# Two-layer graph network on one core: moving the second layer's epilogue one unit later

## The reference

```python
def _L0_gnn_ref(h, adj, W_neigh, b_neigh, W_self, b_self):
    deg = jnp.sum(adj, axis=1, keepdims=True) + 1e-05
    h_neigh = (adj / deg) @ h
    return relu(h_neigh @ W_neigh.T + b_neigh + h @ W_self.T + b_self)

def _L1_gnn_ref(x, adj, W, b):
    d = jnp.where(adj.sum(axis=1) > 0, adj.sum(axis=1) ** (-0.5), 0.0)
    support = (d[:, None] * adj * d[None, :]) @ x
    return relu(support @ W + b)

x = _layernorm(x + _L0_gnn_ref(x, adj, ...))
x = _layernorm(x + _L1_gnn_ref(x, adj, W, b))
```

## Time and profile before

| | |
|---|---|
| profiled execution | 786.03 us, span 784.3 us |
| median of three runs | 786.57 us |
| PE busy | 769.7 us (98%) |
| DVE busy | 719.4 us (92%) |
| ACT busy | 422.7 us (54%) |
| second layer | from about 418 us |
| its inner blocks (1 to 6) | about 448 to 722 us |
| two squarings (line 399), mean of one | 468 ns |
| one normalisation (line 405), mean | 589 ns |

### The profile page before, as it was taken

One profiled execution on the slowest core, in us unless ns is written; L12 is line 12 of the kernel. 1 busy time (PEld: TensorE's weight loads), 2 busy tenths in 40 slices (PEclk: granted clock), 3 DMA queues, 4 the chain that ended last, 5 costly groups with the idle time before them and its releaser, 6 DMA issues.

```text
span 784.3 us, 12479 instructions
## 1 busy us (share of the span) xinstructions
PE 769.7 (98%) x4050; PEld 658.7 (84%) x4050; DVE 719.4 (92%) x1221; ACT 422.7 (54%) x590; POOL 2.6 (0%) x14
## 2 busy tenths in 40 slices
PE   9999999999999999999999999999999999999996
PEld 6888888888888888888888789898888889888886
DVE  6999999999899998999979999998999989899754
ACT  5644644646356463554535646555564665656452
POOL 0000000000000000000000000000000000000000
PEclk9999999999999999999999999999999999999998
DMA  8966574746547466474564655657465565745751
GB/s 299 340 237 196 198 253 164 256 170 213 215 164 249 174 198 231 152 249 170 203 232 155 196 186 189 242 170 260 146 219 202 182 241 166 277 146 192 269 164 52
DMA packets 54206, 161.09 MB, mean 205 GB/s; under 512 B 5024, under 2 KB 18080, under 8 KB 54176
## 3 DMA queue, kind: packets, MB, share of 16 engines
q1 hardware_dynamic: 45680, 151.54, 55.6%
q10 hardware_dynamic: 8352, 9.05, 3.7%
q0 software_dynamic: 144, 0.13, 0.1%
HBM read 152.31 MB, written 8.39 MB: 205 GB/s over the span
## 4 chain that ended last, share of the span: by engine, by line
PE 63%; DVE 19%; issue 10%; ACT 5%; DMA 2%; DVEq 1%; ACTq 0%; SPq 0%
PE ps_main L1091 51%; PE ps_epi L967 5%; DVE lo L565 4%; DVE acc L745 2%; DVE xs L565 2%; PE ps_main L1113 1%; ACT tt L405 1%; DMA raw<-adj_t 1%; DVE acc L742 1%; ACT xs L358 1%; DVE tt L643 1%; ACT hi L358 1%; DVE tt L635 1%; DVE tt L622 1%; DVE ps_main L708 1%
## 5 line engine op out<-in xcount | busy, mean ns | idle before, releaser
L358 ACT ACTIVATE hi<-raw 128x1024 fp32r<-128x1024 f32 x254 | 255.2, 1018 | 139.2 <-PE ps_main L1091 102.4
L565 DVE TENSOR_TENSOR lo<-raw,hi 128x1024 fp32r<-128x1024 f32 x254 | 298.0, 1175 | 21.7 <-ACT hi L358 21.6
L1091 PE MATMUL ps_main<-hi,xs 128*128 128x512 f32 x1120 | 278.9, 391 | 0.4 <-DVE xs L685 0.4
L1091 PEld LDWEIGHTS ps_main<-hi,xs 128*128 128x128 f32 x1120 | 207.4, 188 | 42.5 <-DVE xs L685 0.9
L1091 PE MATMUL ps_main<-lo,xs 128*128 128x512 f32 x560 | 149.7, 389 | 0.0
L848 DVE TENSOR_TENSOR acc<-acc,raw 128x1024 f32<-128x1024 f32 x112 | 136.4, 1218 | 0.0
L1091 PE MATMUL ps_main<-hi,zs 128*128 128x512 f32 x544 | 135.5, 391 | 0.0
L1091 PEld LDWEIGHTS ps_main<-lo,xs 128*128 128x128 f32 x560 | 105.1, 188 | 21.9
L1091 PEld LDWEIGHTS ps_main<-hi,zs 128*128 128x128 f32 x544 | 99.5, 188 | 18.9
L358 ACT ACTIVATE xs<-acc 128x1024 fp32r<-128x1024 f32 (+1 forms) x47 | 49.4, 1051 | 105.0 <-DVE acc L747 92.6
L1091 PE MATMUL ps_main<-lo,zs 128*128 128x512 f32 x272 | 72.7, 389 | 0.0
(11 more groups left out here) (159 smaller groups left out, 786.3 us busy)
## 6 DMA issues: line engine op xcount, KB each, us to landing
raw<-adj_t SPq DMA_DIRECT2D x256, 512.0 KB, 3.3
res<-x_nat SPq DMA_DIRECT2D x11, 512.0 KB, 5.9
xt_sb<-xt SPq DMA_DIRECT2D x8, 512.0 KB, 5.9
x_scratch<-tt ACTq DMA_DIRECT2D x8, 512.0 KB, 4.6
res<-x_scratch SPq DMA_DIRECT2D x8, 512.0 KB, 5.3
out<-tt ACTq DMA_DIRECT2D x7, 512.0 KB, 4.8
tt<-x_nat SPq DMA_DIRECT2D x3, 512.0 KB, 4.8
acc<-x_nat ACTq DMA_DIRECT2D x1, 512.0 KB, 5.1
```

Of the source, the lines that this page charges most:

```text
L358: return act.activation(dst, src, ACT.Copy)
L565: return dve.tensor_tensor(dst, src, hi_part.bitcast(f32), ALU.subtract)
L1091: last = pe.matmul(ps[:, f, :], stationary(layer, part, jt, f), mov[:, slot(u), cols], start=(jt == 0 and i == 0), stop=(jt == JT - 1 and ...
```

## The change

In the second layer every epilogue step from the products on happens one unit later (`w = v - layer`): the products after units 3 and 5 instead of 2 and 4, the DVE tile steps at units 6 to 9, the squarings after units 9 and 11, the root after unit 12, the normalisations after units 14 and 15. The store stays after unit 15. The products no longer run as two wide passes (high and low weight side by side, 512 columns) and one narrow pass on the left half, which left two sums for DVE to scale: they run as three narrow passes of 256 columns onto one sum, as in the first layer, and line 635 goes. The fourth sum of the sub-blocks is taken out of `s_sums` and placed behind `place(u, 2)`, so behind the epilogue's last step of that unit.

```diff
-                if v in (8, 10):
-                    square_tiles(layer, e, parity, v // 2 - 4)
-                if v == 11:
+                w = v - layer
+                if w in (8, 10):
+                    square_tiles(layer, e, parity, w // 2 - 4)
+                if w == 11:
                     act.wait_ge(root_ready, n + 1)
...
-                if v == 13:
+                if w == 13:
                     norm_tile(n, 0)
                     norm_tile(n, 1)
...
-                if v == 14:
+                if w == 14:
                     norm_tile(n, 2)
                     norm_tile(n, 3)
...
-                dve.wait_ge(s_chain, g * 3 + 3)
-                dve.tensor_tensor(s4, a12, s2, ALU.subtract).then_inc(s_ready, 1)
+
+            def s_last_sum(b, parity, u):
+                dve.wait_ge(s_chain, s_index(b, parity, u) * 3 + 3)
+                dve.tensor_tensor(s_sum(parity, u, 3), raw[:, slot(u), 0:HB], s_sum(parity, u, 1), ALU.subtract)\
+                    .then_inc(s_ready, 1)
...
-                if 5 <= v < 5 + TB:
+                if 5 <= w < 5 + TB:
                     if p == 0:
-                        scale_product(layer, n, v - 5, sums=tile_sums(layer, e, parity, v - 5))
-                    if p == 1:
-                        add_second(layer, n, v - 5, tile_sums(layer, e, parity, v - 5))
+                        scale_product(layer, n, w - 5, tile_sums(layer, e, parity, w - 5))
+                    if p == 1 and layer == 0:
+                        add_second(w - 5)
                     if p == 2:
-                        add_residual(n, v - 5)
-                if v in (7, 9) and p == 1:
-                    negate_means((v - 7) // 2)
-                if (v, p) == (11, 0):
+                        add_residual(n, w - 5)
+                if w in (7, 9) and p == 1:
+                    negate_means((w - 7) // 2)
+                if (w, p) == (11, 0):
                     root_argument(n)
...
                     place(u, 2)
+                    if by_seven(layer, b) and u + 1 in SU:
+                        s_last_sum(b, parity, u + 1)
...
-                if u in (2, 4):
-                    if u == 2:
+                w = u - layer
+                if w in (2, 4):
+                    if w == 2:
                         pe.wait_ge(stl_ready, n + 1)
...
-                    for t in (u - 2, u - 1):
-                        if layer == 0:
-                            last = product(ps_epi[:, t, 0:F], slice(t * P, (t + 1) * P),
-                                           lambda part, k: moving_weight(0, part, k))
-                        else:
-                            last = wide_product(t, tile_sums(layer, e, parity, t))
-                        last.then_inc(tile_done, 1)
+                    for t in (w - 2, w - 1):
+                        product(tile_sums(layer, e, parity, t)[:, 0:F], slice(t * P, (t + 1) * P),
+                                lambda part, k: moving_weight(layer, part, k)).then_inc(tile_done, 1)
```

More of the change, by code:

```diff
@@ L545, in _ @@
             layers(act, one_block, last_epilogue)
[L548 removed]
+        LINKS = (5 + 2 + 2 * TB + 4, 1 + TB + 4)
         @block.vector
@@ L613, in degrees, with scale_product @@
                     dve.tensor_scalar(root_in[:, TB:2 * TB], row_sums[:, :], TINY, None, ALU.max)
-            def scale_product(layer, n, t, whole=False, sums=None):
+            def scale_product(layer, n, t, sums):
                 dve.wait_ge(tile_done, n * TB + (t + 1))
@@ L620, in scale_product @@
                     linked()
-                at = slice(F, 2 * F) if layer == 1 and not whole else slice(0, F)
                 ins = dve.scalar_tensor_tensor(
-                    out=tt[:, t, :], in0=(ps_epi[:, t, :] if sums is None else sums)[:, at], scalar=(rdeg, d_cur)[layer][:, t:t + 1],
+                    out=tt[:, t, :], in0=sums[:, 0:F], scalar=(rdeg, d_cur)[layer][:, t:t + 1],
                     in1=(bias0, bias1)[layer][:, :], op0=ALU.mult, op1=ALU.add)
-                if whole:
+                if layer == 1:
                     ins.then_inc(tile_read, 1)
@@ L628, in scale_product, with add_second @@
                     link(ins)
-            def add_second(layer, n, t, sums):
+            def add_second(t):
                 linked()
-                if layer == 0:
-                    ins = dve.tensor_tensor(tt[:, t, :], sums[:, F:2 * F], tt[:, t, :], ALU.add)
-                else:
-                    ins = dve.scalar_tensor_tensor(out=tt[:, t, :], in0=sums[:, 0:F], scalar=d_cur[:, t:t + 1],
-                                                   in1=tt[:, t, :], op0=ALU.mult, op1=ALU.add)
-                ins.then_inc(tile_read, 1)
+                dve.tensor_tensor(tt[:, t, :], ps_epi[:, t, F:2 * F], tt[:, t, :], ALU.add).then_inc(tile_read, 1)
             def add_residual(n, t):
@@ L738, in s_sums @@
                 g = s_index(b, parity, u)
-                a12, a22, a11, a21 = [raw[:, slot(u), i * HB:(i + 1) * HB] for i in range(4)]
-                s1, s2, s3, s4 = [s_sum(parity, u, i) for i in range(4)]
+                _, a22, a11, a21 = [raw[:, slot(u), i * HB:(i + 1) * HB] for i in range(4)]
+                s1, s2, s3 = [s_sum(parity, u, i) for i in range(3)]
                 dve.wait_ge(raw_full[slot(u)], (k0 + (u // RING + 1)) * 16)
@@ L873, in scaled_rows @@
                 def scaled_rows(t):
-                    scale_product(layer, n, t, whole=True)
-                    scale_product(layer, n, t + 1, whole=True)
+                    scale_product(layer, n, t, ps_epi[:, t, :])
+                    scale_product(layer, n, t + 1, ps_epi[:, t + 1, :])
                     add_residual(n, t)
@@ L950, in _ @@
         def _(pe):
[L951 to L960, removed]
             def product(ps, rows, weight):
@@ L990, in epilogue @@
                     last.then_inc(rs_summed, 1)
-                if u in (2, 4):
-                    if u == 2:
+                w = u - layer
+                if w in (2, 4):
+                    if w == 2:
                         pe.wait_ge(stl_ready, n + 1)
-                    if u == 4 and layer == 0:
+                    if w == 4 and layer == 0:
                         pe.wait_ge(rs_copied, e + 1)
-                    if layer == 0 and u == 2:
+                    if layer == 0 and w == 2:
                         pe.wait_ge(wl_ready, 2)
-                    for t in (u - 2, u - 1):
-                        if layer == 0:
-                            last = product(ps_epi[:, t, 0:F], slice(t * P, (t + 1) * P),
-                                           lambda part, k: moving_weight(0, part, k))
-                        else:
-                            last = wide_product(t, tile_sums(layer, e, parity, t))
-                        last.then_inc(tile_done, 1)
+                    for t in (w - 2, w - 1):
+                        product(tile_sums(layer, e, parity, t)[:, 0:F], slice(t * P, (t + 1) * P),
+                                lambda part, k: moving_weight(layer, part, k)).then_inc(tile_done, 1)
             def seven_products(b, parity, u, g0):
```

6 lines of the change are left out of this document (3 added, 3 removed).

## The result

| | median us | runs |
|---|---|---|
| before | 786.3 | 20 |
| changed | 788.69 | 20 |

The ratio is 1.0033, 95% interval 1.0026 to 1.0040: slower by 2.4 us, where 783.8 and a gain of 2.7 were forecast, and outside the range of 779.3 to 787.3. The profiled execution took 789.25 us with a span of 787.6 (786.03 and 784.3 before), so this pair of executions lies 3.2 us apart where the medians lie 2.4 apart.

A forecast was written before the change was run, and what follows sets the result against it. DVE and ACT were taken to bound the inner blocks. Period 1.20, first-block swap 0.12, offset 0.86, narrow products -0.14 and raw wait 0.70 made a gain of 2.74 us: 783.3 profiled, 783.8 median, range 779.3 to 787.3.

The forecast's parts named there:

- DVE and ACT set the pace in the inner blocks, not PE: Inner blocks of the second layer: DVE and ACT's chain takes 46.43 us a block, PE needs only 45.1.
- PE's wait is an offset and comes back inside unit 3: Products after unit 2: wait for `st_lo` moves into unit 3; PE reaches unit 4 earlier by 0.86 us, once.
- Narrow passes cost PE 0.04 a pair: Products on PE: twelve narrow matmuls take 1.43 us for 1.39 before; -0.14 in the sum.
- The walk of DVE's list: DVE's stretches from fourth sum to fourth sum: -0.24 us a block in all, new period 46.19.
- The tail does not move: Store issued about 2 us later, behind the last normalisations, still over a microsecond ahead of its reader.
- Granted clock full if no wait exceeds 1.5: Sign for PE: the granted clock stays full provided none of its waits is longer than 1.5 us.
- The raw piece's wait goes, 0.70: DVE's wait for a raw piece at one block boundary should vanish, as `lo` of unit 15 comes earlier: 0.70 us.
- Rival 1: PE's wait really goes as ACT's work fits in the slack: blocks of 45.19, 8 us gain, 778.5; chance 0.17.
- Rival 3: Later store delays unit 3's raw piece on shared DMA engines: measurably slower from 7.9 us landing, 789.5 at 8.0; chance 0.08.

The follow-up runs named there:

- e3: Kernel before with only the narrow passes onto one sum and line 635 gone, every step left in its unit: 779.31 us, ratio 0.9905.
- e4: Kernel before with only the second layer's epilogue steps one unit later; wide passes, second scaled sum and fourth sum's place kept: 797.65 us, ratio 1.0135.
- e6: Kernel before with only the second layer's store issued earlier, after unit 14's normalisations and ahead of unit 15's rounding: 791.31 us, ratio 1.0054.
- e9: Kernel before with narrow passes, the fourth sum's new place and PE's products after units 3 and 5, DVE and ACT steps unshifted: 778.94 us, ratio 0.9900.
- e8: Kernel before with the narrow passes and the fourth sum's new place, without the shift by one unit: 779.03 us, ratio 0.9901.
- e1: Changed kernel with all four normalisations behind unit 14's rounding, so unit 15's rounding lies between them and the store: 785.28 us, ratio 0.9983.
- e2: Changed kernel with the second layer's seven inner stores on GpSimd's queue, plus a small extra transfer near the start: 788.54 us, ratio 1.0029.
- e5: Changed kernel with the second layer's seven inner stores on GpSimd's queue, without a small extra transfer: 783.32 us, ratio 0.9957.
- e7: Changed kernel with the fourth sum back in its old place: 788.69 us, ratio 1.0026.
- e10: Changed kernel with the squarings of the first two tiles behind unit 10's rounding, not ahead of it: 786.14 us, ratio 0.9997.

## Why the prediction was wrong, point by point

- *DVE and ACT set the pace in the inner blocks, not PE*: right. e3, e4 and e6 each move the join's distance by what was taken from or added to DVE's and ACT's lists, in e3 until PE's own pace is reached.
- *PE's wait is an offset and comes back inside unit 3*: right, by the trace of the changed kernel and by e9. In the first inner block PE starts unit 4 (at 461.69) 6.76 us behind the join, where it was 7.63 before (461.89): 0.87 earlier, for the 0.86 forecast.
- *Narrow passes cost PE 0.04 a pair*: too small to see. In e3 and e8 PE does with them at 44.8 to 44.9 us a block what 45.2 was worked out for.
- *The walk of DVE's list*: right to 0.01 us in four stretches (two of its sums, 5.58 and 5.81, come to 5.56 and 5.83 from the terms given), and with the store off ACT right in the fifth, 46.20 for 46.19.
- *The step that failed* is one clause on the tail: "The tail does not move: the store is issued about 2 us later, behind the last normalisations". It looked at who reads the stored rows and never at what stands behind the store in ACT's own list. In the walk the store had no term at all: between the last two normalisations and `hi` of unit 0 nothing was counted. The store is issued 1.0 us later in its block than before (36.39 behind the join, 35.36 before), and ACT is idle there for 0.8 us, 1.1 at the loop's end. From start to start that is 0.92 x 5 = 4.6 with two times 0.3 on top: 5.2, and the five distances are indeed 236.13 us for 5 x 46.19 = 230.95. For the profiled execution the forecast of 783.3 becomes 788.5 with it; measured is 789.25, and 0.7 of the difference is the later first join. That the medians come out closer still (2.7 less 5.2 is a loss of 2.5, measured are 2.4) is in part luck.
- *Granted clock full if no wait exceeds 1.5*: no wait did and the clock was full, but the length of a wait is not what decides it. e6 has four waits of PE of 1.89 to 1.93 us: behind those that end at 506.00 and 553.21 the granted clock stayed at 1.00, behind the one that ends at 600.43 it was 0.50 from 601.40 on.
- *The raw piece's wait goes, 0.70*: borne out as far as the twelve kernels tell. `lo` of unit 15 comes 7.57 us ahead of the sums of unit 3 in the kernel before, e1, e3, e6, e8 and e9 (7.7 at most where nothing waits), and 4 of their 30 distances have a wait of DVE for a raw piece in them (one each in before, e1, e3 and e9); it comes 8.36 to 9.6 ahead in the changed kernel, e2, e4, e5, e7 and e10, and none of these 30 has one. Each is one execution, so the size of 0.70 is not shown.
- *Rival 1* (the whole wait is won, 778.5): wrong for the change, for the reason given, that ACT's idle time isn't where its work was put. What it describes is e3 and e8 (779.31 and 779.03). *Rival 3* named the store's later issue as the danger, but its transfer and not its place on ACT. Its price, a measurable loss from 0.9 us a period on, was then paid on the engine's own list; that the two sizes agree is luck.

## What to carry to other kernels

When a step is moved, write down for its engine what runs between each two of its instructions, the transfers it issues too, and price an issue that waits for its own engine's last result as a full stop: the wait for the result's end, the issue and the restart, here 0.8 us idle. Keep a piece of unrelated work between a result and the transfer that sends it off. A wait on the busiest engine tells which engine is late, and only shortening that one's list helps: here one removed instruction a tile on DVE, with the narrow passes that made it needless, gave 7 us, and the shift that seemed to remove the wait itself cost 11.

## What the runs showed of the hardware

- A transfer issued by ACT that waits for ACT's own last activation is issued 0.17 us (changed; 0.18 in e6) after that activation's end and occupies ACT's queue for 0.40 us, and the next activation starts 0.23 us behind it (0.13 in e6); if an unrelated activation of 1.05 us is already running, the same issue costs no time at all (before, e1).
- Where a loop's end stands behind such a store, 0.3 us come on top, once every two blocks (changed, e4, e7, e10); with a rounding before it, at most 0.1 (e1, e6). That the loop's end is the cause was not tested by itself.
- A transfer of 128 single numbers from GpSimd's queue took 13.3 us to land, and ACT waited 9.5 us for a raw piece behind it (e2), rounding it 7.3 us later than the changed kernel does. Without the small transfer the delay was gone (e5); whether it was the cause, and how, no run here separates from the other traffic at that place.
- Behind a stand of TensorE of 4.8 us the granted clock was 0.50, the lower level of 1.2 GHz (e2, 54 to 58 us); behind two of four waits of 1.9 us it stayed at 1.00, behind another it was 0.50 (e6).
